# Masked graph attention on one core: the first eight row blocks split into a quarter, a quarter and a half of the columns

## What is computed

```python
def _L0_gnn_ref(h, adj, a):            # N, D = 8192, 256
    h1 = h @ a[:d]
    h2 = h @ a[d:]
    e = jax.nn.leaky_relu(h1 + h2.T, negative_slope=0.01)
    attention = jnp.where(adj > 0, e, NEG_BIG)
    attention = jax.nn.softmax(attention, axis=1)
    return attention @ h

h = jnp.maximum(_layernorm(x, axis=-1), 0.0)
x = x + _L0_gnn_ref(h, adj, L0_gnn_a)
```

## Time and profile before

| | us |
|---|---|
| median of 3 runs | 1688.58 (1687.75 to 1688.63) |
| profiled execution, its own time | 1690.27 |
| profiled execution, span from first to last instruction | 1688.5 |
| TensorE matmul busy | 1630.9 (97%) |
| VectorE busy | 1440.1 (85%) |
| ScalarE busy | 1164.5 (69%) |
| GpSimd busy | 220.4 (13%) |

### The profile page before, as it was taken

The page is one execution under the profiler, slowest core; times in us unless marked ns, Lnnn a source line. Parts: engine busy times, 40 slices in busy tenths (PEclk is TensorE's granted clock), DMA queues, the critical chain, the costliest instruction groups (busy, mean ns, idle before and its releaser), DMA issues.

```text
span 1688.5 us, 40886 instructions
## 1 busy us (share of the span) xinstructions
PE 1630.9 (97%) x13504; PEld 1621.2 (96%) x13504; DVE 1440.1 (85%) x2008; ACT 1164.5 (69%) x1158; POOL 220.4 (13%) x309
## 2 busy tenths in 40 slices
PE   4887999999999999999999999999999999999998
PEld 3777999999999999999999999999999999999998
DVE  6999888888888888888888888888888888888887
ACT  5777766767676666767677676766767676676764
POOL 4667301001010100101010010101001010100100
PEclk9999999999999999999999999999999999999999
DMA  6443455555555555555555555555555455555552
GB/s 199 146 147 112 164 173 182 191 166 185 171 198 174 165 191 167 197 174 187 175 172 186 174 199 168 180 174 185 187 173 184 167 196 174 172 192 167 192 173 88
DMA packets 142672, 294.08 MB, mean 174 GB/s; under 512 B 4928, under 2 KB 5440, under 8 KB 142656
## 3 DMA queue, kind: packets, MB, share of 16 engines
q1 hardware_dynamic: 138336, 278.15, 49.4%
q10 hardware_dynamic: 4320, 15.73, 2.5%
HBM read 285.47 MB, written 8.39 MB: 174 GB/s over the span
## 4 chain that ended last, share of the span: by engine, by line
PE 89%; DVE 8%; issue 2%; DMA 1%; DVEq 0%; ACT 0%; POOL 0%; SPq 0%; ACTq 0%
PE acc L609 28%; PE acc L612 27%; PE acc L611 27%; PE T L567 6%; DVE rep L460 3%; DVE w_lo L481 2%; DVE W L471 1%; DVE bst L442 1%; PE rep L582 0%; DMA r_rep<-in_L_gnn_a_dram 0%; DVE mv L447 0%; DMA xb<-in_x_dram 0%; ACT hb L307 0%; DVE adj_in L552 0%; DVE adj_in L547 0%
## 5 line engine op out<-in xcount | busy, mean ns | idle before, releaser
L609 PE MATMUL acc<-h_hi,w_hi 128*128 (+1 forms) x4096 | 1186.2, 290 | 28.9 <-DVE w_lo L481 28.9
L612 PE MATMUL acc<-h_hi,w_lo 128*128 (+1 forms) x4096 | 1159.2, 283 | 0.0
L611 PE MATMUL acc<-h_lo,w_hi 128*128 (+1 forms) x4096 | 1153.8, 282 | 0.0
L350 ACT ACTIVATE w_hi<-W 128x1024 fp32r<-128x1024 f32 x512 | 540.5, 1059 | 420.3 <-DVE W L471 367.0
L609 PEld LDWEIGHTS acc<-h_hi,w_hi 128*128 128x128 f32 x4096 | 776.3, 190 | 33.5 <-issue 33.1
L471 DVE SCALAR_TENSOR_TENSOR W<-r_rep,g_all,T 128x512 f32<-128x512 int8 (+1 forms) x1024 | 720.1, 745 | 103.3 <-DVE w_lo L481 90.5
L611 PEld LDWEIGHTS acc<-h_lo,w_hi 128*128 128x128 f32 x4096 | 781.1, 191 | 0.2
L612 PEld LDWEIGHTS acc<-h_hi,w_lo 128*128 128x128 f32 x4096 | 777.4, 190 | 0.0
L481 DVE SCALAR_TENSOR_TENSOR w_lo<-W,w_hi 128x1024 fp32r<-128x1024 f32 x512 | 627.7, 1226 | 123.4 <-PE acc L612 109.4
L341 ACT ACTIVATE mask<-adj_in,mhalf 128x2048 fp8e5<-128x2048 int32 x256 | 509.2, 1989 | 24.7 <-issue 23.2
L271 POOL TENSOR_TENSOR xb<-xb,stage 128x256 f32<-128x256 f32 x60 | 41.3, 689 | 1381.6 <-ACT hb L379 1361.3
(11 more groups left out here) (58 smaller groups left out, 277.5 us busy)
## 6 DMA issues: line engine op xcount, KB each, us to landing
adj_in<-in_adj_dram SPq DMA_DIRECT2D x256, 1024.0 KB, 5.2
xb<-in_x_dram ACTq DMA_DIRECT2D x15, 512.0 KB, 3.2
out_dram<-xb ACTq DMA_DIRECT2D x15, 512.0 KB, 2.6
xb<-in_x_dram SPq DMA_DIRECT2D x8, 512.0 KB, 3.3
xo<-in_x_dram SPq DMA_DIRECT2D x8, 512.0 KB, 3.3
adj_in<-in_x_dram SPq DMA_DIRECT2D x1, 512.0 KB, 3.2
out_dram<-adj_in SPq DMA_DIRECT2D x4, 128.0 KB, 1.9
r_rep<-in_L_gnn_a_dram SPq DMA_DIRECT2D x1, 256.0 KB, 6.0
```

Source lines behind the costliest of these rows:

```text
L350: nc.scalar.activation(w_hi[:, k % HL, :], W[:, k % 2, :], ACT.Relu).then_inc(s_hi, 1)
L609: nc.tensor.matmul(acc[:, t, 0:WC], w_hi[:, k % HL, cols], rhs_hi, start=start and u == 0, stop=False)
L611: nc.tensor.matmul(acc[:, t, 0:D], w_hi[:, k % HL, cols], rhs_lo, start=False, stop=False)
L612: last = nc.tensor.matmul(acc[:, t, 0:WC], w_lo[:, k % LL, cols], rhs_hi, start=False, stop=stop and u == 1)
```

## The change

The same 128 iterations are done in another order, in 32 *visits* instead of 16 row blocks. Visits 0 to 7 take row blocks 0 to 7 with the column blocks 0 to 3 (two iterations each). Visits 8 to 15 take row blocks 0 to 7 with column blocks 4 to 7. Then come eight times two visits: the right half (column blocks 8 to 15, four iterations) of row block m, and all sixteen column blocks (eight iterations) of row block m + 8.

- The accumulators of a partial visit are copied to `stage` and stored in a DRAM tensor `part_sums` (528 KB); `load_prior` brings the earlier part back into `xo`, and `add_prior` on GpSimd adds the two (one instruction of 128 x 1032).
- Visit 0 makes h of column blocks 0 to 3. Visits 1 to 12 make block v + 3: statistics in two parts at k = 1 and 2, scores one tile at a time at k = 4 to 7 (k counts the visit's eight pairs), and at the start of the next visit (`made`) the rounding, q*h and h_lo of that block. Only one buffer (`hb`) is used for it.
- For blocks from 4 on, `h_rows` waits for `s_hl` to reach c: for h_lo of the block before, the last thing that GpSimd's list for the visit holds. In GpSimd's list `norm` of the new block stands ahead of `rest_h` of the old one.
- The sum of h for blocks 4 to 15 moves from TensorE to GpSimd (`sum_rows`, four additions of 128 x 256 to a block).
- a is copied once to PSUM (`a_ps`), and the scores read it there and write their unused product to SBUF.
- r goes to DRAM (`store_r`, 16 bytes to a partition) and is loaded spread over all partitions (`load_r`, 256 KB, by SyncE, in the last iteration of the visit before). `lay_out_r` and `copy_r` are gone but for the first block.
- A partition holds other rows of adj than before: row t*128 + p of a block instead of 4p + t. The pieces of 2 KB are the same; those of one partition are now 128 rows (4 MB) apart, and those of neighbouring partitions one row (32 KB). The rows of x for the result and of out follow, in pieces of 1 KB.
- In visit 0, `subtract(g)` follows W of the same pair, and every block's scores are cut in two.

```diff
+            def quarter(v, q, prev, make=False, made=False, nxt=None, head=False, turn=False):
+                visit(Visit(v=v, n0=2 * v, b=v - SH * q, c0=Q * q, its=Q // CI, prev=prev,
+                            pb=SH - 1 if turn else v - 1 - SH * q, f=None,
+                            pa=v - SH - 1, make=v + 3 if make else None,
+                            made=v + 2 if made else None, ...
+            quarter(0, 0, None, head=True)
+            quarter(1, 0, "first", make=True)
+            with eng.Fori(2, SH - 1) as v:
+                quarter(v, 0, "first", make=True, made=True)
...
+            with eng.Fori(SH + 1, NB - 3) as v:
+                quarter(v, 1, "added", make=True, made=True)
...
# SyncE
+            def load_r(V):
+                if V.head:
+                    sp.wait_ge(s_aps, 1)
+                    sp.wait_ge(s_dot, 2 * G * Q + 2)
+                    sp.wait_ge(s_rd, 16 * 2)
...
+                sp.dma_start(r_rep[:, (V.v + 1) % 2, :], r_dram[ds(V.nxt, 1), :].partition_broadcast(P)).then_inc(
+                    s_rr, 16)
...
+                    load_adj(V.b, c + kc, n, kc, not (V.head and first))
+                    if V.make is not None and first and kc == 0:
+                        load_more_x(V.make)
+                    if V.nxt is not None and last and kc == (1 if V.head else 0):
+                        load_r(V)
# GpSimd
+                if V.made is not None and first:
+                    scale_h(V.made, 0)
+                    sum_rows(V.made)
+                if V.prev in ("added", "rest") and first:
+                    add_prior(V)
+                if V.make is not None and first:
+                    norm(V.make, 0)
+                if V.made is not None and first:
+                    rest_h(V.made, 0)
+                if V.prev in ("full", "rest") and last:
+                    for t in range(G):
+                        finish(V.f, t)
# ScalarE, h_rows
+                    if isinstance(c, int) and c < Q:
...
+                    else:
+                        act.wait_ge(s_hl, c)
# ScalarE, side_work(V, k), behind w_hi of pair k
+                if V.made is not None:
+                    if k == 0:
+                        round_h(V.made, 0, [0, 1])
+                    if k == 2:
+                        round_h(V.made, 0, [2, 3])
+                        store_r(V.made)
+                if V.prev is not None:
+                    if k == 1:
+                        evacuate(V)
+                if V.make is not None:
+                    if k == 3:
+                        h_rows(V.make, 0, [0, 1])
+                    if k == 4:
+                        h_rows(V.make, 0, [2, 3])
+                    if k == 7:
+                        exps(V.make, 0)
+                if V.prev in ("first", "added") and k == 4:
+                    store_part(V)
+                if V.prev in ("added", "rest") and k == 0:
+                    load_prior(V)
+                if V.prev in ("full", "rest"):
...
+                    if k == 6:
+                        normalise(V.f, 2)
+                        normalise(V.f, 3)
+                    if k == 7:
+                        store_out(V)
# VectorE, side_work(V, k), between w_lo and W of pair k
+                if V.make is not None:
+                    if k == 1:
+                        stats(V.make, 0, V.make - 1, [0, 1])
+                    if k == 2:
+                        stats(V.make, 0, V.make - 1, [2, 3])
+                    if k >= 4:
+                        scores(V.make, 0, [k - 4])
```

More of the change, by code:

```diff
@@ L3 @@
 from contextlib import ExitStack
+from collections import namedtuple
+Visit = namedtuple("Visit", "v n0 b c0 its prev pb f pa make made nxt head tail")
 def masked_graph_attention(nc, x, adj, a, out):
@@ L188, in iteration @@
-                if last and first_block:
-                    sp.wait_ge(s_z, NB)
-                    sp.sem_inc(s_stored, 16)
-            run(sp, iteration)
+                    if V.head and not first:
+                        load_x(c + kc, kc, True)
+                    load_adj(V.b, c + kc, n, kc, not (V.head and first))
[3 more added lines that the diff above has]
+                        load_r(V)
@@ L421, in iteration @@
-                if last and first_block:
-                    act.wait_ge(s_hsum, NB)
-                    act.wait_ge(s_hl, NB)
-                    nc.scalar.activation(hmean, hs_ps[:, 0:D], ACT.Copy, scale=1.0 / N).then_inc(s_mean, 1)
-                if last and not first_block:
-                    store(b - 1)
-                if first and not first_block and not last_block:
-                    copy_r(b + 1)
-            run(act, iteration)
+                    h_rows(0, 0, range(G))
+                    h_rows(1, 1, range(G))
@@ L450, in scores @@
-            def scores(c, parity):
-                h = h_bufs[parity]
-                dve.wait_ge(s_z, c + 1)
-                if not isinstance(c, int) or c > 1:
-                    dve.wait_ge(s_ex, c - 1)
-                out = head_junk if isinstance(c, int) and c < 1 else junk
-                for e in range(G):
+                if 0 in tiles:
+                    dve.wait_ge(s_x[parity], 16 * loaded)
+                    if not isinstance(c, int) or c > 1:
+                        dve.wait_ge(s_rs, c - 1 if isinstance(c, int) and c < Q else c)
@@ L466, in weights @@
                 dve.wait_ge(s_T, c_tot + 1)
-                if not early:
+                if wait:
                     dve.wait_ge(s_lo, g - 1)
```

567 lines of the change are left out of this document (329 added, 238 removed).

## The result

| | before | after |
|---|---|---|
| median, us (5 runs each, taken together) | 1688.63 (1687.75 to 1689.73) | 1696.58 (1694.33 to 1702.01) |
| ratio, 95% interval | | 1.0054 [1.0035, 1.0074] |
| profiled execution, span and own time, us | 1688.5 and 1690.27 | 1692.5 and 1694.33 |

The forecast was 1681.5 with a range of 1663 to 1700: the time is in the range, but on the other side of no change. It lies at the rival to which I gave 0.07 (1695, *final visits pay at their seam*).

What follows compares the result with a forecast made beforehand. TensorE bounds the kernel, except VectorE in the first row block. 90.4 + 11 x 28.9 = 408.3; with 7.5, 415.8; with 1257.7 and 6.0, 1679.5; with 2 for final visits, 1681.5 us; range 1663 to 1700.

Steps and rivals of the forecast that it cites:

- final visits pay at their seam: Rival, chance 0.07: at the ends of visits that also finish a block, 1 us lost at each of 15, 1695.
- Costed at nothing: Accumulator copies, DMAs and GpSimd's sum taken as hidden; late normalisations in the sixteen final visits given 2 us in all.
- the stage before: Visits up to 12, in which h is made: TensorE was to end them at 415.8 us.
- Wait for h_lo: Visits 2 to 12: scores wait for h, held by the block before's h_lo; 28.3 or 29.75 us, 28.9 taken.
- no wait: Rival, chance 0.20: ScalarE and GpSimd run further ahead, visits that make h take 27.2 us, total 1663.
- The bound of 31.5: Upper bound in us for each of visits 2 to 12: 29.75 and one drop of the clock.
- Exclusion, the reading of the earlier trace: GpSimd instructions and VectorE ones with two SBUF inputs (w_lo) exclude each other, instruction by instruction; h_lo stretched to 2.94 from 2.18.
- Sum on GpSimd: The sum of h, 0.69 us each on GpSimd, was to be done before `norm` can start, so cost nothing.
- Visit 0: First visit: adj for visit 1 issued only after the last score, lands at 57; the mask waits, visit 1 starts at 66.
- adj slower: Rival, chance 0.03: adj loads take twice the time, 10.4 us, as one partition's pieces lie 4 MB apart; 13 us, 1694.

Runs made afterwards that it cites:

- the combined kernel: The changed kernel with the store one visit later, h_rows not waiting for h_lo, and r of visit 1 loaded behind adj; 1654.09 us, ratio 0.9789.

## Why the forecast failed, step by step

- **The step that failed** is the last one of *Costed at nothing*: "w_hi of the last pair and the next mask 1.5 to 2.3 late, against some 2 of slack: I add 2 us in all." The lateness of the mask was sized well (1.7 us). The slack was not: no row of mine shows it. The mask's transposes stand in TensorE's own list ahead of the last pair's products, and TensorE reached them with 0.4 us to spare. The step also names only the two additions between the normalisations, and not the store that waits for the last addition ahead of the mask; with the store moved, the late w_hi alone cost nothing. The term was some 18 us (14 seams at (100.2 - 98.65 + 50.39 - 49.32)/2 = 1.3), not 2. Without it the span would be 1692.5 - 18 = 1674.5. The run with the later store has 1677.9; of the difference, 2.4 us lie in visits 2 to 12, which end at 413.45 there instead of 411.07 (visit 9 took 32.67 us against 30.12), and 0.6 in its one full visit of 99.27.
- **The chances.** The rival had this mechanism and nearly its price (1 us at 15 seams, measured 1.3 at 14), and got 0.07, since I set it against a slack that I had not read from any row. The kernel before has the same place in every row block, and TensorE does not idle there; that shows that a seam without a double normalisation fits, and nothing on one with it. That the median of 1696.58 lies so near to the rival's 1695 is in part luck: the stage before was 4.7 us shorter than forecast, and the median is 2.3 us above the profiled execution.
- **Wait for h_lo: right in kind.** 27.6 to 28.1 us in visits 2 to 8 and 29 to 30.2 in 9 to 12 are a mean of 28.6 against 28.9. It came out so near by luck, since two terms inside were off and cancelled. VectorE alone needs less than my 27.2: pairs with scores follow each other in 3.14 us (162.46, 165.60, 168.73), where I had 3.4. And the exclusion between w_lo and h_lo costs VectorE 1.85 us in most visits beside the wait for h of 0.90; I had let it only shift the scores. The bound "no wait", 27.2, was measured at 26.95, of which 1.85 are that exclusion. The bound of 31.5 has a drop of the clock at 1.7 us, for which I had no row; 3.4 us at a clock of 0.50 in after are 1.7 us of TensorE's work, of which a visit paid some 1.1 (last section).
- **Exclusion, the reading of the earlier trace rows: shown** by the run with h_lo in pieces, and by the run with the short sum, where the engine that comes first is the one that is not held. (The rows themselves I had read loosely: the score ends at 35.61, 0.3 and not 0.1 us after h_lo.) By the rule of the Trainium skill on the interfaces (GPSIMD Engine Reference, Specifications) that I had cited, the trace agrees: w_lo, with two inputs in SBUF, went from 1.22 to 3.07 us; the scores, with an input in PSUM, took 0.39 to 0.42 in all of after.
- **Sum on GpSimd, costed at nothing: wrong where it could be measured.** On top of the combined kernel, leaving most of it out saved 9.4 us (1654.09 to 1644.74). What it cost in the changed kernel itself no run shows.
- **Visit 0: right.** adj is late and the mask waits. VectorE begins visit 1 at 64.94, forecast 66, and visit 2 at 88.02, forecast 90.4.
- **adj slower: refuted.** 5.4 us to landing against 5.2. The rule of the Trainium skill (DMA: Bandwidth & Descriptors, Latency and other measured facts) is on neighbouring partitions' rows 4 MiB apart. Here it is the pieces of one partition that lie so far apart, so these runs do not test it.

## What to carry to other kernels

Before a stall is called covered, read the waiting engine's own list: what it must do next, and which of its inputs stands behind the stall, not only the input that has spare buffers. A transfer issued by a computing engine is an instruction with a wait; put it where its data have long been ready, behind what another engine needs. An engine that is busy for a fifth of the time can still set the pace: cut its long instructions where the other engine is in a hurry, and leave them whole where its own list is.
